# A two-stream decoder on one core: the last gated attention computed another way, the first loads, the bias rows, the function tables and the orders of work changed

## What is computed

```python
qkv = concatenate([x, ctx, ctx], -1)
ig = qkv @ igate_kernel + igate_bias            # [B, S, 8]
fg = qkv @ fgate_kernel + fgate_bias
cs = cumsum(log_sigmoid(fg))
log_D[s, t] = cs[s] - cs[t] + ig[t] if t <= s else -inf
D = exp(log_D - max_t(log_D))                   # max over the keys t
C = (q @ k.T / sqrt(16)) * D
h = (C / (max(abs(sum_t C), exp(-max_log_D)) + 1e-6)) @ v
out = layernorm_per_head(h) * outnorm_weight
```

## Time and profile before

| | us |
|---|---|
| median of 3 runs | 1081.8 (1080.71 to 1082.05) |
| the profiled execution: time | 1080.39 |
| its span, first to last instruction | 1078.4 |
| PE busy (matmul) | 921.6 (85%) |
| PEld busy (weight load) | 687.3 (64%) |
| DVE busy | 570.5 (53%) |
| ACT busy | 440.2 (41%) |
| POOL busy | 47.4 (4%) |
| mean granted clock of TensorE | 0.93 of 2.4 GHz |

### The profile page before, as it was taken

One profiled execution on the slowest core, in us unless ns is written; L12 is line 12 of the kernel. 1 busy time (PEld: TensorE's weight loads), 2 busy tenths in 40 slices (PEclk: granted clock), 3 DMA queues, 4 the chain that ended last, 5 costly groups with the idle time before them and its releaser, 6 DMA issues. The chain is left out here.

```text
span 1078.4 us, 20461 instructions
## 1 busy us (share of the span) xinstructions
PE 921.6 (85%) x8328; PEld 687.3 (64%) x8328; DVE 570.5 (53%) x1589; ACT 440.2 (41%) x897; POOL 47.4 (4%) x68
## 2 busy tenths in 40 slices
PE   6689899899988898988778978988998888898782
PEld 4246578778877584666426745876888766784441
DVE  5744535654356376364554864665425458364347
ACT  2036415354554462361224333533355553632332
POOL 0300000000010000000000000001001000000000
PEclk9699979999999998995969999999999999999875
DMA  9000000301001101121000000030100110000000
GB/s 336 27 2 1 2 2 1 157 2 36 1 18 57 76 1 40 41 88 55 1 1 12 1 2 2 2 156 2 35 2 19 60 73 2 1 1 1 1 1 19
DMA packets 6829, 35.97 MB, mean 33 GB/s; under 512 B 721, under 2 KB 4305, under 8 KB 5458
## 3 DMA queue, kind: packets, MB, share of 16 engines
q1 hardware_dynamic: 6738, 34.68, 8.7%
HBM read 34.15 MB, written 0.52 MB: 32 GB/s over the span
## 5 line engine op out<-in xcount | busy, mean ns | idle before, releaser
L660 PE MATMUL bank<-xT,weights_F 128*128 128x256 f32 x832 | 201.9, 386 | 0.7 <-DVE small L1285 0.7
L660 PEld LDWEIGHTS bank<-xT,weights_F 128*128 128x128 f32 x832 | 152.5, 193 | 23.6 <-issue 4.3
L668 PEld LDWEIGHTS bank<-weights_F,p 128*128 128x128 f32 x1088 | 133.9, 192 | 16.8 <-issue 5.6
L668 PE MATMUL bank<-weights_F,p 128*128 128x128 f32 x1088 | 140.6, 278 | 3.2 <-ACT p L1890 2.3
L1742 ACT ACTIVATE p<-bank 128x512 f32<-128x512 f32 x160 | 84.0, 602 | 115.4 <-PE bank L506 101.4
L1330 DVE SCALAR_TENSOR_TENSOR res<-bank,comb,res 128x128 f32<-128x128 f32 x184 | 55.9, 345 | 74.7 <-PE bank L668 72.5
L1814 ACT ACTIVATE p<-bank 128x512 f32<-128x512 f32 x72 | 42.9, 598 | 99.1 <-PE bank L660 98.6
L1171 DVE TENSOR_REDUCE m_wide<-bank 128x4 f32<-128x512 f32 x96 | 60.3, 683 | 43.1 <-PE bank L767 35.3
L1346 DVE TENSOR_TENSOR p<-p,bank 128x512 f32<-128x512 f32 x72 | 49.3, 685 | 49.1 <-PE bank L660 26.8
L1890 ACT ACTIVATE p<-bank 128x512 f32<-128x512 f32 x64 | 36.5, 598 | 44.6 <-PE bank L660 44.5
L1179 DVE TENSOR_REDUCE mx<-bank 128x4 f32<-128x512 f32 x64 | 39.9, 682 | 27.8 <-PE bank L500 27.6
(11 more groups left out here) (323 smaller groups left out, 1441.5 us busy)
## 6 DMA issues: line engine op xcount, KB each, us to landing
weights_F<-in_L1f SPq DMA_DIRECT2D x2, 4096.0 KB, 13.2
weights_F<-in_L0f SPq DMA_DIRECT2D x2, 3456.0 KB, 13.1
weights_F<-in_L2f SPq DMA_DIRECT2D x2, 3456.0 KB, 11.4
weights_Y<-in_L1x_kv SPq DMA_DIRECT2D x2, 1024.0 KB, 10.3
weights_Z<-in_L1x SPq DMA_DIRECT2D x2, 1024.0 KB, 11.3
weights_Y<-in_L2a SPq DMA_DIRECT2D x2, 898.0 KB, 4.5
weights_Z<-in_L2x SPq DMA_DIRECT2D x2, 449.0 KB, 3.5
weights_L3m<-in_L3m SPq DMA_DIRECT2D x2, 288.0 KB, 6.2
```

The source lines that it names most:

```text
L660: m = mm(b[:, k * NT:(k + 1) * NT], W[weight][:, f:f + P], s.xT[:], start=True, stop=True)
L668: m = mm(b[:, tk(u)], h[:, tk(u)], w, start=k == 0, stop=k == len(chunks) - 1)
```

## The change

- **Gates.** The two context thirds of the gate weights are added once by GpSimd (both thirds multiply the same context). Each gate has a bank of its own, opened in L3a's tail; the context's 4 matmuls are issued there, before x is turned, and only x's 4 follow in L3x.
- **Keys spread by ScalarE.** The spreading of x by the head mask moves from VectorE (2 instructions of 512 columns) to ScalarE (4 of 256, with the mask as scale), ahead of the softplus.
- **Maxima.** The block-diagonal product and its matmul of 512 columns go; in their place 4 matmuls of 128 columns per unit, with one column of `pick` broadcast as the stationary operand and the row of maxima moving.
- **Retrieval turned.** The values, padded with ones to 32 columns, are stationary, the probabilities move (128 columns); ScalarE copies the result out and TensorE turns it back, 4 heads at a time. VectorE reads PSUM directly: no `keep`.
- **Tables.** ScalarE's loads for silu and the gelus are issued by the program through `use`, ahead of the wait for the bank, and only if another set is loaded.
- **Start.** xT of a and the weights of L0a are loaded ahead of the constants, xT of b just behind; the context by token comes late. TensorE waits for the constants at its first transpose and for the masks in L0x. GpSimd zeroes `vz`. The bias rows are spread after stream b's L0a output matmul, in three steps; VectorE copies them in two.
- **Unused parts** (`warm`, `ones_bf`, `zeros_bf`) go.
- **Orders.** The orders of TensorE, VectorE, ScalarE and GpSimd are new throughout. Near the end TensorE's order was: a and b L3a projections, turns, gates of a, gates of b, transposes, then units and retrievals of a and b in turn. It becomes: a's projection, context gates, turn, b's last L3a values, a's gates and first units, b's projection and context gates, a's last units, b's turn, a's first retrieval, b's gates, the rest of a, and then b's transposes, units, retrievals and turns back.

The core of the diff (12 columns of indentation taken off):

```diff
+        if pair == 1:
+            rows = lambda a, e: s.p[0:1].rearrange("p a b -> p (a b)")[:, a:e]
+            pe.wait_ge(*weights("rows"))
+            b = opened("act", "rows", 2)
+            for k in range(2):
+                m = mm(b[:, k * D:(k + 1) * D], rows(896 + k * D, 896 + (k + 1) * D), ones_row, start=True, stop=True)
+            filled(m, "rows", 2)
+            yield
+            filled(mm(opened("dve", "rows", 0)[:], ones_row, rows(0, 512), start=True, stop=True), "rows", 0)
+            yield
+            b = opened("dve", "rows", 1)
+            mm(b[:, 0:384], ones_row, rows(512, 896), start=True, stop=False)
+            pe.wait_ge(*ready("small"))
+            pe.wait_ge(*ready("L3a"))
+            pe.wait_ge(*freed("rows", 2))
+            mm(b[:, 128:256], s.kT[:, 0:T], W["L2x_o"], start=False, stop=False)
+            filled(mm(b[:, 256:384], s.kT[:, T:2 * T], W["L3a_o"], start=False, stop=True), "rows", 1)
+            yield
...
             values8("L3a", u, [(0, probs_of(u))])
             yield
         project("L3a", W["L3a_o"])
-        yield from tail("L3a")
+        yield from tail("L3a", lambda: gate_logits_of("L3x", 1, s.ctxT))
+
+    def gate_logits_of(st, k, src):
+
+        if k:
+            if turn == 0:
+                pe.wait_ge(S("L3x_context_gates"), 1)
+            pe.wait_ge(*ready(st))
+        for part in range(2):
+            b = opened("dve", st, "gates", part) if k else ring.bank((pair, st, "gates", part))
+            for u in range(NS):
+                a = 16 * k + 8 * part
+                m = mm(b[rows32(u), 0:T], W["L3x_gates32"][:, a:a + 32], src[:, tk(u)], start=k == 1, stop=k == 0)
+            if not k:
+                filled(m, st, "gates", part)
 
     def L3x():
-        pe.wait_ge(*ready("L3x"))
         pe.wait_ge(*freed("L3a", "xT"))
-        b = opened("dve", "L3x", "gates")
-        for part in range(2):
-            for k in range(3):
-                for u in range(NS):
-                    a = 16 * k + 8 * part
-                    m = mm(b[rows32(u), part * T:part * T + T], W["L3x_gates32"][:, a:a + 32],
-                           (s.ctxT if k else s.xT)[:, tk(u)], start=k == 0, stop=k == 2)
-        filled(m, "L3x", "gates")
-        yield
-        yield
+        gate_logits_of("L3x", 0, s.xT)
         yield
 
...
-                filled(mm(heads(b[:], 4), const("ones")[rows32(u), 0:T], s.m_diag8[rows32(u), 4 * half:4 * half + 4],
-                          start=False, stop=True), "L3x", "D", i)
+                for j in range(4):
+                    h = 4 * half + j
+                    m = mm(b[:, j * T:j * T + T], const("pick")[rows32(u), h:h + 1].to_broadcast([32, P]),
+                           s.gates[rows32(u), 5], start=False, stop=j == 3)
+                filled(m, "L3x", "D", i)
 
         def retrieved(u):
-            b = opened("dve", "L3x", "o", u)
+            b = opened("act", "L3x", "oT", u)
             for half in range(2):
                 pe.wait_ge(*freed("L3x", "s", 2 * u + half))
                 for j in range(4):
-                    h = 4 * half + j
-                    m = mm(b[:, 17 * h:17 * h + 17], s.p[:, 2 * u + half, j * T:j * T + T], s.v17[:, u, h],
-                           start=True, stop=True)
+                    m = mm(b[rows32(j), half * T:half * T + T], s.v_ones[:, u, 4 * half + j],
+                           s.p[:, 2 * u + half, j * T:j * T + T], start=True, stop=True)
+            filled(m, "L3x", "oT", u)
+
+        def turned_back(u):
+            b = opened("dve", "L3x", "o", u)
+            pe.wait_ge(*freed("L3x", "oT", u))
+            for half in range(2):
+                m = tr(b[:, half * T:half * T + T], s.qk[:, u, half * T:half * T + T], IDENT)
             filled(m, "L3x", "o", u)
...
-        pe.wait_ge(*told("L3x_bd", NS))
-        pe.wait_ge(*told("L3x_m_diag"))
+        pe.wait_ge(*told("L3x_bd"))
         units(0, 3)
...
+        turned_back(0)
+        yield
+        turned_back(1)
+        yield
...
-pe.wait_ge(*weights("con"))
-pe.wait_ge(S("masks"), 5)
 take_turns("pe", program)
```

VectorE, ScalarE, GpSimd and SyncE:

```diff
-        b = bank("L3x", "gates")
         for part, bias in enumerate(("L3x_ib", "L3x_fb")):
-            done = o.count(dve.tensor_scalar(gt[:, part], b[0:64, part * T:part * T + T], W[bias][0:64], None, ALU.add),
-                           free("L3x", "gates") if part else None)
+            b = bank("L3x", "gates", part)
+            done = o.count(dve.tensor_scalar(gt[:, part], b[0:64, 0:T], W[bias][0:64], None, ALU.add),
+                           free("L3x", "gates", part))
         dve.wait_ge(*done)
         link(dve.scalar_tensor_tensor(gt[:, 5], gt[:, 1], -1.0, gt[:, 1], ALU.mult, ALU.min), sem("L3x_absf"))
-        yield
-        spread_heads(s.bd_c, s.xT, sem("L3x_bd"), mask16)
         yield
         dve.wait_ge(*told("L3x_softplus"))
         ones = const("ones")[0:64, 0:T]
...
         link(dve.tensor_tensor_scan(gt[:, 5], ones, gt[:, 2], -3.0e38, ALU.mult, ALU.max))
         link(dve.tensor_tensor(gt[:, 4], gt[:, 3], gt[:, 5], ALU.add), sem("L3x_gates"))
         yield
-        o.count(dve.scalar_tensor_tensor(s.m_diag8, among(gt[:, 5], 8), -1.0, over(const("delta8")[0:64], T),
-                                         ALU.mult, ALU.mult), sem("L3x_m_diag"))
-        for u in range(NS):
-            o.count(dve.tensor_copy(s.v17[:, u, :, 0:DC], heads(s.ctx_tok[:, u], HC)), sem("L3x_v17") if u else None)
+        for u in range(NS):
+            o.count(dve.tensor_copy(s.v_ones[:, u, :, 0:DC], heads(s.ctx_tok[:, u], HC)), sem("L3x_v") if u else None)
...
-        held = s.qs[:].rearrange("p u d -> p (u d)"), s.ks[:].rearrange("p u d -> p (u d)")
-
-        def keep(u):
-            b = bank("L3x", "o", u)
-            return o.count(dve.tensor_copy(held[u][:, 0:HC * 17], b[:, 0:HC * 17]), free("L3x", "o", u))
-
-        for i in (0, 3, 1):
+        for i in (0, 3, 1, 2):
             unit(i)
             yield
-        keep(0)
-        yield
-        unit(2)
-        yield
         n, m = s.small[:, :, 0:8], s.small[:, :, 8:16]
-        done = keep(1)
+        out = [heads(bank("L3x", "o", u)[:, 0:NT], HC) for u in range(NS)]
+        dve.wait_ge(*freed("L3x", "mx"))
+        minus = [o.count(dve.scalar_tensor_tensor(n[:, u], out[u][:, :, DC], -1.0, s.small[:, u, 32:40], ALU.mult, ALU.max))
+                 for u in range(NS)]
+        for u in range(NS):
+            dve.wait_ge(*minus[u])
+            done = o.count(dve.tensor_tensor(n[:, u], out[u][:, :, DC], n[:, u], ALU.max))
         dve.wait_ge(*done)
-        out = [heads(x[:, 0:HC * 17], HC) for x in held]
-        for u in range(NS):
-            o.count(dve.scalar_tensor_tensor(n[:, u], out[u][:, :, DC], -1.0, out[u][:, :, DC], ALU.mult, ALU.max))
-        dve.wait_ge(*freed("L3x", "mx"))
-        o.settle()
-        link(dve.tensor_tensor(n, n, s.small[:, :, 32:40], ALU.max))
         link(dve.tensor_scalar(n, n, 1e-6, None, ALU.add))
         link(dve.reciprocal(n, n))
         h = s.xb[:].rearrange("p u (h d) -> p u h d", h=HC)
         for u in range(NS):
-            done = o.count(dve.tensor_tensor(h[:, u], out[u][:, :, 0:DC], over(n[:, u], DC), ALU.mult))
-        dve.wait_ge(*done)
+            done = o.count(dve.tensor_tensor(h[:, u], out[u][:, :, 0:DC], over(n[:, u], DC), ALU.mult), free("L3x", "o", u))
+        for u in range(NS):
+            dve.wait_ge(*freed("L3x", "o", u))
...
-for s in streams:
-    dve.memset(s.vz[:], 0.0).then_inc(S(f"zeroed_{s.g}"), 1)
 dve.wait_ge(*weights("con"))
-for dst, src in ((ident_bf, IDENT), (neg_causal_bf, const("neg_causal")), (neg_causal_t_bf, const("neg_causal_t")),
-                 (ones_bf, const("ones"))):
+for dst, src in ((ident_bf, IDENT), (neg_causal_bf, const("neg_causal")), (neg_causal_t_bf, const("neg_causal_t"))):
     dve.tensor_copy(dst[:], src).then_inc(S("masks"), 1)
...
+def use(functions):
+
+    if table[0] != functions:
+        act.preload_act_table_set(functions)
+        table[0] = functions
+
 def exp_ln():
-
-    if table[0] != EXP_LN:
-        act.preload_act_table_set(EXP_LN)
-        table[0] = EXP_LN
+    use(EXP_LN)
...
-            table[0] = "silu"
+            use("silu_and_others")
             b = bank(st, "gate", e)
...
         gt = s.gates
         exp_ln()
+        act.wait_ge(*ring.freed((pair, "L3a", "xT")))
+        for j in range(4):
+            o.count(act.activation(s.bd_c[:, :, j], by_sample(s.xT[:]), ACT.Identity,
+                                   scale=const("head16in64")[:, j:j + 1]), sem("L3x_bd") if j == 3 else None)
+        yield
         act.wait_ge(*told("L3x_absf"))
         link(act.activation(gt[:, 5], gt[:, 5], ACT.Exp))
...
+        for u in range(NS):
+            keep("L3x", ("oT", u), s.qk[:, u])
+            yield
...
             pool.wait_ge(*weights("L1a"))
             o.count(pool.tensor_scalar(neg_bb[:], W["L1a_bb"][0:64], -1.0, None, ALU.mult), S("neg_bb"))
             latent_mats()
```

(53 more changed lines are left out.)

41 lines of the change are left out of this document (17 added, 24 removed), and 54 rows, old and new, of the table TURN_ORDER.

## The result

The changed kernel takes 1053.89 us (median of 4 runs, 1045.37 to 1056.96) where the kernel before, run beside it, takes 1081.92: a ratio of 0.9721, 95% interval 0.9658 to 0.9784. The forecast was 1057. The total is right; its parts, as the experiments show, are mostly not.

What follows compares the result with a forecast made beforehand. TensorE's work was taken to bound the long middle, chains of short dependent steps both ends. Terms -6 - 5 - 12 - 2 = -25 us from 1080.39 gave 1055.4, plus 1.4 for the median: 1057 us, range 1043 to 1071.

Steps and rivals of the forecast that it cites:

- The start, -6: Up to the first x_tok: moved loads, zero fills and bias rows save 6 us, ends -9 and -2.
- what leaves that chain leaves the total: First 87 and last 67 us: a chain of short dependent steps sets the time, so whatever is removed from it shortens the total.
- The first turn's gated attentions, -5: Gated attentions beside the other stream's work: TensorE loses 13 us of work, 5 us of it felt, ends -8 and 0.
- The end, -12: Last gated attentions, from b's x_tok at 1014.6 us to the last x_tok: 12 us shorter, ends -16 and -6.
- a ahead of b, taken as 5: Last turn: stream a's gated attention going ahead of stream b's is 5 us of the end's 12.
- The prices: TensorE per four pairs of samples: retrieval -18.3, turning back +3.7, gates -3.7, maxima +5, in all -13 us.
- the slower rival: Turned retrieval makes in-order TensorE wait eight times for ScalarE's copy, 3.8 us each: +30, so 1087 us; chance 8%.
- The table loads, -2: ScalarE: ten fewer function-table loads, 12.8 us of its time, shorten the total by 2 us, ends 0 and -6.
- TensorE idles 15% of the span, so that share is felt: Table loads: of the 12.8 us ScalarE saves, only TensorE's idle share of 15% counts, giving -2 us.
- All orders redone, 0: The two long stretches with 78 us of TensorE idle: new orders counted as 0, since no row prices them.
- the ends of -8 and +12: Limits of the orders term: a tenth less idle in the long stretches, or 15% more.
- the order gains too: Rival: 10% less idle in the middle, table loads at -6 and start at -8 give 1044 us; chance 18%.

## Why the prediction was right in total and wrong in its parts

- **The start, -6.** The marks came as forecast (first x_tok at 16.90, the output matmul at 9.61 instead of 17.30 in the earlier trace rows). The loads, fills and waits are worth 5 us (0.5 to 10) in the order of before and about 2 in the new one; stream a's x of layer 0's cross-attention is turned at 84.7 to 88.3 us in the four traces of the changed kernel, against 85.8 before. The bias rows weren't measured alone. The failing step is "what leaves that chain leaves the total" as applied to the start. Beyond 87 us TensorE's work is the bound, and what is gained ahead of it counts only as far as TensorE gets more done: 67.35 us in the first 87 with the change, 66.70 with its start undone, 62.05 with its code in the orders of before, 61.82 before. It is the order that fills the room.
- **The first turn's gated attentions, -5.** Not settled. Against the traces with the attention or one part of it undone, the changed kernel is 2.7 to 4.1 us shorter there in its trace at the same low clock, and 7 to 9 in its three others; but the kernel before takes 116.3 us in one trace and 108.3 with only its start changed. A gain of 5 is in the midst of that.
- **The end, -12.** The stretch is 10.7 us shorter (91.0 to 80.3) in the first trace, in the size of the term, and 5.5 to 7.4 in the three others, short of the term's end of -6 in two. The granted clock is in it: between a's and b's turned x of L3a the first trace has it at 1.00 and takes 16.5 us (988.04 to 1004.58), the next one at a mean of 0.75 and takes 20.1. Its halves were wrong: a ahead of b, taken as 5, isn't distinguishable from nothing, and the rebuild alone gives 3.5 in the order of before and 17 to 22 in the new one. Without the rebuild the new order makes the end 11 us longer (102.3 against 91.0). The forecast priced the two as a sum; they pay only together.
- **The prices.** Maxima 15.0 us (taken 14 to 16), turning back 4.1 (3.7), the gates' two groups 5.5 where three took 12.2 (-6.7, taken -3.7), retrieval 5.9 (4.5). By these groups TensorE has 14.6 us less work; 13 were forecast, and in all 3.9 less are seen. Part of the rest is the granted clock: L666, whose 832 instructions are the same, went from 201.9 to 205.3, and in the run at 0.943 TensorE was busy 911.5 us, 10 less than before. The waits of TensorE for the turned result stayed under 2 us at a time (1.7 in all at L1058), so the slower rival's mechanism, 3.8 us each, isn't there. Of the Trainium skill's rule on weight loads (TensorE: Matmul & The Clock Gate, The mechanism), by which the maxima would cost 10 us more: 16 records, two units in one group of rows each, took 1.71 us at full clock, 107 ns each with a weight load each, and while only one unit was running its records began 111 ns apart. The trace speaks for overlap here.
- **The table loads, -2.** The count was one off (68 besides the last, 77 before: besides the 65 through `use`, three by the compiler at L1810, L1970 and L1971). The step "TensorE idles 15% of the span, so that share is felt" failed: a load added costs 0.82 us, and nine make 7 us if a load removed is worth what one added costs, beyond the term's end of -6. That wasn't measured: no run takes loads away by itself. By the Trainium skill (ScalarE: Activation LUTs, What ACT_TABLE_LOAD costs) the term would have been -4; the load itself lasts 1283 ns in every trace, as the page has it, and of the drain that the page adds these traces show nothing: behind 48 of the 69 the next instruction begins 11 or 12 ns after the load.
- **All orders redone, 0.** This is the wrong step. "No row prices it: 0" stood for 24 us, the table loads' 7 and the bias rows' move among them; the ends of -8 and +12 didn't hold the 17 that remain without the loads. The rival "the order gains too" (18%) named the mechanism, at half its size.

So of the 28 us (26 at equal clock, by the lines through both kernels' runs), 24 hang on the orders, and the forecast's -25 came from terms that without them bring 6. The sizes met by luck of signs: start, end and attention were given too much by themselves, orders and tables too little. The shares are no sum: undoing the orders costs 24 us, and undoing the attention in the new orders another 12 to 19 of the same 28. What is shown is that the new code needs the new orders; that the new orders with the old attention already have most of the gain before the end is shown too (17.8 us ahead at 955 us, the changed kernel 16.1 to 28.5 in its four traces), and that at the end they are a loss without it.

## What to carry to other kernels

Where two streams fill each other's gaps in a written-out order, an edit has no price of its own: price it together with the order, and look in the waits for how often the in-order engine is sent to work that isn't ready (here 15 times, then 8). Don't take function-table loads for free because ScalarE is idle more than half the time: an added one cost two thirds of its length here. A gain ahead of a stretch bound by throughput was worth little here beyond the work pulled into it. And compare two variants at the same granted clock, or over several traces: one stretch of one kernel differed by 5 us from trace to trace, as much as most terms of the forecast.

## What the runs showed of the hardware

- An fp32 product with 128 columns of probabilities moving past 32 stationary columns, four heads side by side, took 5.9 us for 128 records (46 ns each), the same product with 128 stationary and 17 moving columns 21.6 to 22.8 us (169 to 178 ns each). With 128 stationary and 128 moving columns, L668 took 129 ns a record: few moving columns saved nothing. How much of the 46 ns is the narrow weight load and how much the four side by side, no run separates.
- A record with its weights broadcast from one column took 107 ns at a granted clock of 1.00 (2.4 GHz) and 193 at 0.50 (3.09 us for 16), no more than L668's 129 at its mixed clock.
- Two identical table loads in a row are one load in the trace; with a load of another table ahead both are there, and each takes 1283 ns.
- The changed kernel, untouched, ran between 1042.6 and 1060.6 us over four sets, at mean granted clocks of 0.950 and 0.927 in those two runs; a line through all 22 runs gives 7 us for each 0.01.
